# Attention in steps of two pairs of heads: both pairs' scores in one run, two pairs' transposes in one run, four PSUM banks shared

## The reference, cut to what matters

```
h = layernorm(x)
h = layernorm(h + attention(h, h,   mask)) * g + b      # self-attention
h = layernorm(h + attention(h, ctx, mask)) * g + b      # cross-attention
h = layernorm(h + gelu(h @ fc1 + b1) @ fc2 + b2) * g + b
x = x + h
out = x + geglu(layernorm(x), shared) + geglu(layernorm(x), W[expert chosen per row])

attention(x, ctx, mask):
    q, k, v = x @ wq, ctx @ wk, ctx @ wv                # split in 16 heads
    p = softmax(q @ k.T / 8, with masked columns at the lowest float)
    return (p @ v, heads side by side) @ wo + bo
```

## Time and profile before

| what | value |
|---|---|
| median of 3 runs | 1231.66 us (1231.28 to 1233.45) |
| the profiled execution | 1231.06 us, its span 1229.3 us |
| PE busy in the span | 1213.4 us (99%) |
| DVE, ACT, POOL busy | 990.7 (81%), 880.8 (72%), 700.0 us (57%) |
| granted clock of TensorE | 1.0 over the span |

### The profile page before, as it was taken

The page is one execution under the profiler, slowest core; times in us unless marked ns, Lnnn a source line. Parts: engine busy times, 40 slices in busy tenths (PEclk is TensorE's granted clock), DMA queues, the critical chain, the costliest instruction groups (busy, mean ns, idle before and its releaser), DMA issues.

```text
span 1229.3 us, 31384 instructions
## 1 busy us (share of the span) xinstructions
PE 1213.4 (99%) x10412; PEld 1162.4 (95%) x10412; DVE 990.7 (81%) x2676; ACT 880.8 (72%) x2272; POOL 700.0 (57%) x1098
## 2 busy tenths in 40 slices
PE   8999999999999999999999999999999999999998
PEld 6999999999999999999999999999999999999898
DVE  6888888888989988888888889754554888888964
ACT  6988888788888888888888887644333776777642
POOL 5766656656668856555555577886533222334452
PEclk9999999999999999999999999999999999999999
DMA  6060000000000003200000010010023688877822
GB/s 197 5 247 19 19 1 19 12 8 19 10 19 27 2 28 128 72 28 27 2 27 28 2 36 27 19 61 27 1 97 106 212 274 263 263 250 251 265 81 95
DMA packets 74383, 100.60 MB, mean 82 GB/s; under 512 B 5616, under 2 KB 53616, under 8 KB 74224
## 3 DMA queue, kind: packets, MB, share of 16 engines
q1 hardware_dynamic: 72688, 94.40, 23.6%
q0 software_dynamic: 1536, 4.20, 1.1%
HBM read 84.16 MB, written 14.42 MB: 80 GB/s over the span
## 4 chain that ended last, share of the span: by engine, by line
PE 84%; DVE 6%; ACT 5%; issue 3%; DMA 1%; SPq 0%; DVEq 0%; ACTq 0%
PE ps_pj L52 9%; PE ps_pj L54 9%; PE ps_pj L53 9%; PE ps_t L965 8%; PE ps_s L955 8%; PE ps_pv L978 8%; PE ps_aux L54 4%; PE ps_aux L52 4%; PE ps_aux L53 4%; ACT probs L1289 4%; PE ps_s L52 4%; PE ps_s L54 4%; PE ps_s L53 4%; PE ps_pv L52 2%; PE ps_pv L54 2%
## 5 line engine op out<-in xcount | busy, mean ns | idle before, releaser
L668 POOL TENSOR_SCALAR probs<-probs,inv 128x256 f32<-128x256 f32 x512 | 235.7, 479 | 220.8 <-DVE inv L1538 220.2
L1289 ACT ACTIVATE probs<-scores,nb 128x256 f32<-128x256 f32 x512 | 253.6, 497 | 16.6 <-DVE nb L1528 16.1
L1528 DVE CUSTOM_DVE_ANT_0 scores<-ps_s,maskf 128x256 f32<-128x256 f32 x512 | 186.7, 420 | 53.9 <-PE ps_s L955 51.5
L1296 ACT ACTIVATE probs_t_hi<-ps_t 128x512 fp32r<-128x512 f32 x256 | 150.9, 590 | 99.3 <-PE ps_t L965 99.3
L1542 DVE TENSOR_TENSOR probs_t_lo<-ps_t,probs_t_hi 128x512 fp32r<-128x512 f32 x256 | 173.1, 676 | 0.4
L965 PE MATMUL ps_t<-ident,probs 128*128 128x128 f32 x1024 | 139.9, 279 | 0.6 <-POOL probs L668 0.6
L978 PE MATMUL ps_pv<-probs_t_lo,v_stack 128*128 128x256 f32 x512 | 130.3, 287 | 1.1 <-issue 1.0
L978 PE MATMUL ps_pv<-probs_t_hi,v_stack 128*128 128x256 f32 x512 | 127.7, 282 | 0.0
L965 PEld LDWEIGHTS ps_t<-ident,probs 128*128 128x128 f32 x1024 | 109.7, 141 | 17.7 <-POOL probs L668 0.9
L52 PE MATMUL ps_pj<-xq_hi,wq_lo 128*128 128x256 f32 x368 | 115.0, 312 | 0.1
L687 POOL TENSOR_TENSOR heads_t_lo<-joined,heads_t_hi 128x256 fp32r<-128x256 f32 x128 | 95.0, 742 | 30.7 <-ACT heads_t_hi L1305 30.3
(11 more groups left out here) (293 smaller groups left out, 4476.5 us busy)
## 6 DMA issues: line engine op xcount, KB each, us to landing
raw<-in_L_ffn_W SPq DMA_DIRECT2D x96, 512.0 KB, 5.0
slot_rows<-hin SPq DMA_DIRECT2D x3, 768.0 KB, 6.2
rows<-in_x SPq DMA_DIRECT2D x8, 256.0 KB, 2.7
after_self<-rows SPq DMA_DIRECT2D x8, 256.0 KB, 2.1
rows<-after_self SPq DMA_DIRECT2D x8, 256.0 KB, 2.7
cin<-in_ctx SPq DMA_DIRECT2D x8, 256.0 KB, 3.0
after_cross<-rows SPq DMA_DIRECT2D x8, 256.0 KB, 2.5
stage<-in_L_xattn_fc_w SPq DMA_DIRECT2D x2, 1024.0 KB, 9.0
```

The costliest lines, as they stand in the source:

```text
L668: last = pool.tensor_scalar(PR[:, h, t, :], PR[:, h, t, :], inv[:, h, t:t + 1], 1.0, ALU.mult, ALU.mult)
L1289: last = act.activation(PR[:, h, t, :], SM[:, h, t, :], ACT.Exp, bias=nb[:, h, t:t + 1], scale=-1.0, accum_out=sums[:, h, t:t + 1])
L1296: act.activation(flat(PT[0][:, i % 2, h, :, :]), ps_t[h][:, :], ACT.Copy).then_inc(t_hi, 1)
L1528: last = dve.tensor_tensor_reduce(SM[:, h, t, :], ps_s[h][:, t * S:(t + 1) * S], maskf[:, i // PAIRS % 2, :], -SCALE, -LOWEST, ALU.add, AL ...
```

## The change

Attention goes in steps of two pairs, i = 2k. PE does scores(i+2) and scores(i+3) in one run, then project_qk(i+4), attend(i), project_v, the transposes of pairs i+1 and i+2 in one run, project_qk(i+5), output of two pairs, sometimes a transposition of rows, attend(i+1). Scores and transposed probabilities share the four banks ps_s and ps_t: even pairs have their scores in ps_s and their transposes in ps_t, odd pairs the other way round. masked_max writes into the buffer of the probabilities, of which there are three, and exps works in place; `scores` as a buffer goes. nb, sums and inv are doubled. The lists of DVE, ACT and POOL are rewritten to the step, and the pieces of the weights are converted at other places.

```diff
             def scores(i):
                 pe.wait_ge(pj_lo, EVENT[("qk", i)] + 1)
-                wait(pe, max_ready, 2 * i)
+                if i == 2:
+                    pe.wait_ge(t_lo, 2)
+                elif i == 3:
+                    pe.wait_ge(max_ready, 4)
+                elif i > 3:
+                    pe.wait_ge(t_lo, 2 * (i - 2))
...
             def transpose_probs(i, h):
                 pe.wait_ge(norm_ready, 2 * i + h + 1)
-                wait(pe, t_lo, 2 * (i - 1) + h + 1)
+                if i == NPAIR - 1:
+                    pe.wait_ge(t_lo, 2 * (i - 2) + h + 1)
+                elif i >= 1:
+                    pe.wait_ge(max_ready, 2 * (i + 1) + h + 1)
...
+            def scores_bank(i, h):
+                return (ps_t if i % 2 else ps_s)[h]
+
+            def turned_bank(i, h):
+                return (ps_s if i % 2 or i == 0 else ps_t)[h]
...
+            for k in range(TURNS_OF_TWO):
+                i = 2 * k
+                scores(i + 2)
+                scores(i + 3)
+                if i + 4 < NPAIR:
+                    project_qk(i + 4)
+                attend(i)
+                project_v(k + 1)
+                if k == TURNS_OF_TWO - 1:
                     transpose_first(0)
...
+                for n in (i + 1, i + 2):
+                    transpose_probs(n, 0)
+                    transpose_probs(n, 1)
+                if i + 5 < NPAIR:
+                    project_qk(i + 5)
+                if k >= 1:
+                    output(i - 2)
+                    output(i - 1)
+                if turn_rows(k) is not None:
+                    what, u = turn_rows(k)
+                    (transpose_ctx if what == "xc" else transpose_rows)(u)
+                attend(i + 1)
...
                 dve.wait_ge(s_done, 2 * i + h + 1)
                 dve.sem_inc(dve_gate, 1)
-                if i >= 1:
-                    dve.wait_ge(exp_ready, 2 * (i - 1) + h + 1)
+                if i >= 2:
+                    dve.wait_ge(exp_ready, 2 * (i - 2) + h + 1)
+                    dve.sem_inc(dve_gate, 1)
+                if i >= 3:
+                    dve.wait_ge(t_done, 2 * (i - 3) + h + 1)
                     dve.sem_inc(dve_gate, 1)
```

DVE's list of a step, and ACT's, without the parts that come in single steps only:

```diff
+                masked_max(i + 2, 0)
+                masked_max(i + 2, 1)
+                if k >= 1:
+                    join_pair(i - 1)
+                invert_sums(i + 2, 0)
+                masked_max(i + 3, 0)
+                invert_sums(i + 2, 1)
+                masked_max(i + 3, 1)
+                if i + 4 < NPAIR:
+                    lo_of_bank(("qk", i + 4))
+                join_pair(i)
+                invert_sums(i + 3, 0)
...
+                lo_of_bank(("v", k + 1))
...
+                lo_of_probs(i + 1, 0)
+                lo_of_probs(i + 1, 1)
+                lo_of_probs(i + 2, 0)
+                lo_of_probs(i + 2, 1)
+                invert_sums(i + 3, 1)
+                if i + 5 < NPAIR:
+                    lo_of_bank(("qk", i + 5))
```

```diff
+                if k >= 1:
+                    cross_of_pair(i - 1)
+                exps(i + 2, 0)
+                exps(i + 2, 1)
+                if i + 4 < NPAIR:
+                    hi_of_bank(("qk", i + 4))
+                if k >= 1:
+                    hi_of_pair(i - 1)
+                cross_of_pair(i)
+                exps(i + 3, 0)
+                hi_of_bank(("v", k + 1))
...
+                hi_of_probs(i + 1, 0)
+                hi_of_probs(i + 1, 1)
+                hi_of_pair(i)
+                hi_of_probs(i + 2, 0)
+                hi_of_probs(i + 2, 1)
+                exps(i + 3, 1)
+                if i + 5 < NPAIR:
+                    hi_of_bank(("qk", i + 5))
+                if turn_rows(k) is not None:
+                    hi_of_bank(turn_rows(k))
```

More of the change, by code:

```diff
@@ L74, in layer_of, with turn_rows @@
     return u // B
-def bank_events():
[L79 to L90, removed]
+def turn_rows(k):
+    u = k // STEPS_PER_TURN + 1
+    if u < NTURN and k % STEPS_PER_TURN == 0 and layer_of(u):
+        return ("xc", u)
+    if u < NTURN and k % STEPS_PER_TURN == 1:
+        return ("xq", u)
+    return None
@@ L128, in set_of @@
+PIECES_AT = {start + at: pieces for start, plan in zip(STARTS, PIECES_IN) for at, pieces in plan.items()}
 def set_of(i):
-    return sum(i >= base for base in BASES[1:])
+    return sum(i >= start for start in STARTS[1:])
 LATE = [(0, kind, q) for kind, q in AHEAD] + [(set_of(j), kind, q) for j in sorted(PIECES_AT) for kind, q in PIECES_AT[j]]
@@ L288, in fused @@
         OT = at("heads_t_hi", 140 * KB, [P, 4, S], F32R), at("heads_t_lo", 148 * KB, [P, 4, S], F32R)
-        SM = at("scores", 152 * KB, [P, 2, ST, S])
-        PR = at("probs", 156 * KB, [P, 2, ST, S])
+        PR = [at(f"probs{r}", (152, 156, 132)[r] * KB, [P, 2, ST, S]) for r in range(3)]
         XQ = [(at(f"xq{r}_hi", (160 + 4 * r) * KB, [P, KC, S], F32R), at(f"xq{r}_lo", (162 + 4 * r) * KB, [P, KC, S], F32R))
@@ L314, in fused @@
         mhalf = little("mhalf", [P, ST])
-        nb, sums, inv = (little(n, [P, 2, ST]) for n in ("nb", "sums", "inv"))
+        nb, sums, inv = (little(n, [P, 2, 2, ST]) for n in ("nb", "sums", "inv"))
         part, mv = little("part", [P, 3, ST, 6]), little("mv", [P, 3, ST, 2])
@@ new lines, in _ @@
+            scores(1)
+            project_qk(2)
+            transpose_probs(0, 0)
+            transpose_probs(0, 1)
+            project_qk(3)
+            for k in range(TURNS_OF_TWO):
+                i = 2 * k
+                scores(i + 2)
[4 more added lines that the diff above has]
+                project_v(k + 1)
+                if k == TURNS_OF_TWO - 1:
+                    transpose_first(0)
+                for n in (i + 1, i + 2):
[10 more added lines that the diff above has]
+                attend(i + 1)
@@ L1210, in _ @@
+            up_dense(0, 0)
+            attend(NPAIR - 2)
+            up_dense(0, 1)
+            transpose_probs(NPAIR - 1, 0)
+            transpose_probs(NPAIR - 1, 1)
+            output(NPAIR - 4)
+            output(NPAIR - 3)
+            attend(NPAIR - 1)
+            transpose_step(1)
+            up_dense(0, 2)
+            up_dense(0, 3)
+            output(NPAIR - 2)
+            output(NPAIR - 1)
             down(0, range(FC))
@@ new lines, in _ @@
+            masked_max(1, 0)
+            masked_max(1, 1)
+            invert_sums(1, 0)
+            lo_of_bank(("qk", 2))
+            lo_of_probs(0, 0)
+            invert_sums(1, 1)
+            lo_of_probs(0, 1)
+            lo_of_bank(("qk", 3))
+            for k in range(TURNS_OF_TWO):
+                i = 2 * k
+                u, p = k // STEPS_PER_TURN, k % STEPS_PER_TURN
+                masked_max(i + 2, 0)
+                masked_max(i + 2, 1)
+                if k >= 1:
+                    join_pair(i - 1)
[7 more added lines that the diff above has]
+                invert_sums(i + 3, 0)
+                if p == 1 and u >= 1:
+                    residual_sum(u - 1)
+                lo_of_bank(("v", k + 1))
+                if k == TURNS_OF_TWO - 1:
+                    lo_of_bank(("h", 0))
+                lo_of_probs(i + 1, 0)
[5 more added lines that the diff above has]
+                    lo_of_bank(("qk", i + 5))
+                if turn_rows(k) is not None:
+                    lo_of_bank(turn_rows(k))
+                late_hi_pieces(k)
+                if k == PAIRS:
```

243 lines of the change are left out of this document (95 added, 148 removed), and 10 rows, old and new, of the table PIECES_IN.

## The result

The changed kernel takes 1275.09 us (median of 4 runs, 1274.46 to 1276.71), the kernel before beside it 1231.47 us (4 runs, 1231.07 to 1233.45). The ratio is 1.035, 95% interval 1.034 to 1.037: slower by 43.6 us, where I had forecast 20.5. The profiled execution has a span of 1273.9 us, 44.6 more than the one before.

What follows compares the result with a forecast made beforehand. PE, 99% busy, was taken as the bound; each step gains 0.30 us at borders and loses 0.63 waiting for the join, so 1231.06 + 20.5 + 0 for the rest gives 1252 us, range 1238 to 1272.

Steps and rivals of the forecast that it cites:

- The borders: On PE, entering and leaving the scores' run costs 0.38 us a two-pair step instead of 0.68, a gain of 0.30.
- The wait for the join: Before attend(i), DVE's chain of 3.01 us against PE's cover of 2.46 makes PE lose 0.63 us a step.
- the count of t_done: The added wait with a count ahead of masked_max on DVE costs 0.11 us, bounded by 0 and 0.11.
- The sum of it: Attention's step grows by 0.33 us to 11.85, 62 times: +20.5 us.
- What else moves: Late statistics and casts against shrinking waits for the lows of q and k: set equal, bounds -4 and +8 us.
- The order of the weights' pieces: Converted weight pieces are asked for no earlier than PE has them; no cost.
- Some of the 5.8: Of PE's 5.8 us of waits for the lows of q and k, some occur at the start in either order.
- Casts and statistics: On DVE, where row or context transposes meet output_stats or weight casts, work comes late: 2 to 10 us in all.
- the loads that hang on them: Loads that hang on POOL's moved steps have a whole step of time.
- The end of attention: up_dense(0, 0) between the last attends gives cover enough: 0 us, within 2.
- Rival one: The join does not hold PE before attend, only the borders count: 18.6 us faster, 1213 us, chance 0.13.
- Rival two: ACT and DVE become the bound, their loop put at 10.9 us against a step of 11.85: 1270 us, chance 0.12.

Runs made afterwards that it cites:

- e3: Changed kernel with masked_max's waits and counts for exp_ready and t_done put ahead of its wait for s_done: 1265.62 us, ratio 1.028.
- e4: Changed kernel with three pieces of the output's weights converted one step earlier in the first turn: 1267.42 us, ratio 1.030.
- e8: Changed kernel with pair 0's transposes in two idle banks (ps_pv, ps_aux) instead of ps_s: 1275.95 us, ratio 1.035.
- e7: Changed kernel with the context of turn 11 loaded ahead of the dense weights instead of behind them: 1274.0 us, a single execution.
- e1: Changed kernel with join_pair(i-1) ahead of masked_max(i+2) in DVE's list: 1272.64 us, ratio 1.033.
- e2: Changed kernel with project_v(k+1) ahead of attend(i) in PE's list: 1267.57 us, ratio 1.029.
- e6: Changed kernel with e1's order, DVE's casts and output statistics behind the join, e4 and e7 together: 1242.70 us, ratio 1.009.
- e11: e6 with e8, e3 and POOL's last steps reordered, then pair 127's low part of the heads moved earlier on POOL: 1240.97 us, ratio 1.008.
- e5: Changed kernel with DVE's weight casts and output_stats moved behind the next step's masked_max and join, and join_pair(125) ahead of the last casts: 1276.24 us, ratio 1.036.

## Why the prediction was right in sign and too small

**The borders.** Right. 0.38 a step was forecast; the rows give 0.21 + 0.22 into and 0.21 + 0.22 out of the run, less 4 x 0.12, 0.38. A run twice as long costs no more at its end.

**The wait for the join.** Right, term by term: 0.69 forecast and measured (0.58 + 0.11) to masked_max, 1.39 (1.38) to the join, 0.84, and 0.10, 3.02 against 3.01; PE stands 0.56 and loses 0.07 to fill again, 0.63. A step is 11.84 (11.85), 62 times. That the count of t_done costs 0.11 on an idle DVE was a choice between 0 and 0.11, and e3 settles it: two counts moved away give 0.22.

**The sum of it.** 52 ordinary steps gave 17.9 us, 0.34 each, so 62 would give 21.4 where 20.5 stood.

**The step that failed** is the term "What else moves": "I set the two equal, bounds -4 and +8". By the table it is 44.6 - 20.5 = 24 us, three times the upper bound. In the prediction's own sentences:

- "The order of the weights' pieces asks for nothing earlier than PE has it." Wrong. wo's first pieces come to POOL at 47.41 and 63.86, where output wants them at 46.1 and about 63; e4 gives 7.7 us for these two. I had checked the order of the list and not the time of each piece against its use.
- "Some of the 5.8 are at the start, where the first pairs wait in either order", taken as a credit. At the start the new order loses: up to attend(0) 2.6 us, with one clock fall in them. e8 shows that the shared bank by itself is not what holds it; its two stands point to the order of the scores.
- Casts and statistics "2 to 10 us in all". This loss is there and within its size: a step with a transposition is 12.44, 0.15 over the sum of its parts, and four weights' steps lose 5.1 beyond the ordinary 0.33, with one clock fall (1.7) in them. What was wrong is what I set against it. The waits for the lows of q and k did shrink, from 5.8 us to 1.3 (the 1.0 above and 0.3 at 13 us), but of the 5.8 only some 3.4 lay behind 80 us, and where the rest was, at the start, the new order has longer stands instead.
- "the loads that hang on them have a whole step". Wrong once: cin, 1.7 us, by e7.
- "The end of attention has up_dense(0, 0) between the last attends, cover enough: 0, within 2." Wrong: 5.4 us beyond the ordinary loss. attend(124) stands 3.08 and attend(126) 2.25. For attend(124) my cover of 2.46 us isn't there: the last step of the loop has no project_qk(i + 4), twelve matmuls or 1.4 us, as the condition in the diff says. The first pair's last score matmul is at 789.35, the last of all at 790.06, and the casts and the statistics hold DVE on top of it:

```profile
791.10 0.42 DVE L1573 CUSTOM_DVE_ANT_0 probs<-ps_s,maskf 128x256 f32<-128x256 f32 x1
```

This is 1.75 behind the scores instead of 0.69. DVE and POOL at attend(126), in the timelines of the changed kernel:

```profile
802.13 1.29 DVE L1536 CAST wq_hi<-stage 128x512 fp32r<-128x512 f32 x1
803.34 1.48 DVE L1536 CAST wo_hi<-stage 128x512 fp32r<-128x512 f32 x1
804.74 0.84 DVE L1596 TENSOR_TENSOR joined<-ps_pv,cross 64x256 f32<-64x256 f32 x2
```

```profile
801.85 1.29 POOL L716 TENSOR_TENSOR wv_lo<-stage,wv_hi 128x512 fp32r<-128x512 f32 x1
803.10 1.44 POOL L716 TENSOR_TENSOR wq_lo<-stage,wq_hi 128x512 fp32r<-128x512 f32 x1
```

At attend(126) two casts stand ahead of the join, and last 1.29 and 1.48 instead of 0.41 while POOL works on tensors of the same size.

- The clock stood in no term at all. I had read 1.0 in every slice before and carried it over. Long stands can cost twice: once themselves, once by the slow pitch behind them, 1.7 us for each of six, up to 10.2 of the 24 us (of these 3.4 are taken back by e4, with the stands). The forecast stands of half a microsecond left it at 1.0; the falls all come behind stands that I had priced at nothing.

**The rivals.** Rival one (1213) is excluded: the stand is there, and e1 shows that even without it the time isn't 1213. Its sum left out that DVE's work has to be somewhere. Rival two was put at 10.9 against 11.85; e2 shows the loop at 11.73 in its order, so it was nearer than I had it. The loop isn't one number: in e1 and e6 the plain steps run at 11.3 to 11.4, and the step with a transposition and the one behind it bring the four of a turn to 47.6 and 46.7 us, against 46.7 in the kernel before. There DVE and ACT wait for each other, as the rows of e1 show, and this keeps the repairs small. By itself: the Trainium skill, TensorEngine Tiling (Array Packing), PSUM Bottleneck, says that tiling does not speed up the emptying of PSUM, which may then bind. The runs agree, with 36 waits for the lows of q and k in e2.

**What stays open.** How the remaining 0.8% of e11 is shared is read only from its trace (up to attend(8) +5.7, weights' steps +3.8, from attend(122) on +5.5, the stretches between -4.4); I did not bring any of these down further. Nor was the place of output_stats tried by itself. And why one long stand is followed by a fall of the clock and another of the same length is not, these runs don't show.

## What to carry to other kernels

A reordering that is right in the steady state is priced there, but lost at the seams: for each hand-over at the start, at the end and in the steps with extra work, put the time at which the operand is ready beside the time at which PE wants it, and don't let a list's order stand for its times. When one wait is taken out, ask for the next bound before counting the gain; in e2's order it lay 0.12 us a step behind. And for a stand of some 2 us or more on TensorE ask what the slow clock behind it would cost: here it mostly came, at 1.7 us or more.

## What the runs showed of the hardware

- The granted clock. In the changed kernel PE waited 2.25 to 3.1 us ahead of each of the six falls. In the traces of all twelve new kernels there are 46 waits of 2.25 us or more (from 14 us on), and 42 have a fall beside or behind them; waits of 1.5 us (533 us) and 1.7 us (399 us) in the changed kernel have none, and no fall in these traces, but for the last one at the kernels' end, stands without a wait of 1.80 us or more. Between the two it goes both ways: 2.1 us (e5, 415 us) and 2.0 us (e11, 783 us) left the clock at 1.00, and 1.80 us in e8 (534 us) had a fall behind it (0.82 and 0.76 in the two windows). The length doesn't decide it alone: the 3.08 us ahead of attend(124) were followed by a fall in the changed kernel and left the clock at 1.00 in e4 (784 to 792 us), as did 3.25 us in e1 (66 us) and 2.75 in e2 (796 us). In e8 a wait of 1.97 us that came 2.9 us behind one of 0.80 was followed by a fall as well (0.74 from 24 to 28 us). A fall cost 1.7 us in the changed kernel, and 3.4 behind the wait of 3.18 us in e1 (0.71, 0.50 and 0.94 from 800 to 812 us). By itself: the Trainium skill, TensorE: Matmul & The Clock Gate, What's actually happening, describes a gate with the two levels of 1.2 and 2.4 GHz. The trace agrees, with a pitch of 0.21 against 0.12.
- DVE's cast of 128x512 from SBUF takes between 0.41 and 1.55 us (32 of them). The eight of over 1 us all lie beside 1.2 us or more of a TENSOR_TENSOR on POOL, as at 802 us; those at 395.57 and 395.90, where POOL is idle, take 0.41, and so do three that lie beside POOL's TENSOR_SCALAR alone (424, 777 and 789 us). That POOL is the cause was not isolated.
- A semaphore wait with its count on an idle DVE costs 0.11 us even if it is met long before (e3: two of them, 0.22).
